# An MoE layer's 64 experts written out instead of looped, eleven weight buffers instead of eight, and row gathers signalled by pairs

## The reference

```python
logits = x @ gate_weight.T;  scores = softmax(logits)          # 64 experts in 8 groups of 8
# 3 groups with the highest maxima, then the 6 best experts inside them
slot = flat * C + jnp.minimum(pos, C - 1)                       # C = 96 rows per expert
buf = jnp.zeros((E * C, H)).at[slot].set(x[tok]).reshape(E, C, H)
g = einsum('ech,emh->ecm', buf, Wg);  u = einsum('ech,emh->ecm', buf, Wu)   # M = 176
out = einsum('ecm,ehm->ech', silu(g) * u, Wd)
y = sum(out[slot] * topk_w) + silu(x @ Sg.T) * (x @ Su.T) @ Sd.T
```

## Time and profile before

| what | before |
|---|---|
| three runs | 1605.34, 1607.7, 1599.73 us; median 1605.34 |
| the profiled execution's own time | 1592.39 us |
| its span, first to last instruction | 1590.4 us |
| mean granted TensorE clock | 0.932 |

### The profile page before, as it was taken

How to read it: one execution, slowest core, us unless ns; L and a number is a source line. 1 busy time by engine, 2 the same in 40 slices (tenths; PEclk the granted TensorE clock), 3 DMA queues, 4 the chain that set the end, 5 groups by cost and what they waited for, 6 DMA issues and landing times. The chain is left out here.

```text
span 1590.4 us, 35813 instructions
## 1 busy us (share of the span) xinstructions
PE 1382.2 (87%) x13732; PEld 971.8 (61%) x13733; DVE 1121.4 (71%) x2131; ACT 676.9 (43%) x1430; POOL 737.9 (46%) x811
## 2 busy tenths in 40 slices
PE   3849999997679999999999999999986976999832
PEld 2424545445546777777777777777765545888731
DVE  4867888876767898788878887887764687222229
ACT  1226777772144555555555555555541110222200
POOL 0341111100338697667666766676650027677610
PEclk9968999999779999999999999999997888999965
DMA  3052000000116988788788887887783300799838
GB/s 107 1 233 86 2 2 2 2 2 1 54 51 126 160 154 142 142 152 152 140 137 155 146 145 135 157 142 145 136 151 109 92 1 15 232 281 281 256 121 266
DMA packets 423530, 191.39 MB, mean 120 GB/s; under 512 B 377507, under 2 KB 397697, under 8 KB 423249
## 3 DMA queue, kind: packets, MB, share of 16 engines
q1 hardware_dynamic: 404576, 164.08, 49.1%
q0 software_dynamic: 6144, 12.52, 2.7%
q10 hardware_dynamic: 12656, 12.72, 2.5%
HBM read 73.91 MB, written 23.13 MB: 61 GB/s over the span
## 5 line engine op out<-in xcount | busy, mean ns | idle before, releaser
L941 POOL CAST a_ph<-a_p 128x1024 f16<-128x1024 f32 (+7 forms) x256 | 248.8, 972 | 232.4 <-ACT a_p L1087 232.3
L1137 DVE TENSOR_TENSOR a_ph<-a_p,a_ph 128x1024 f16<-128x1024 f32 (+7 forms) x256 | 259.6, 1014 | 14.5 <-POOL a_ph L941 14.4
L1087 ACT ACTIVATE a_p<-bank,a_negm 128x1024 f32<-128x1024 f32 (+7 forms) x256 | 188.9, 738 | 125.3 <-DVE a_negm L1154 124.9
L1047 PE MATMUL bank<-a_v,a_pt 128*128 128x128 f16 x3456 | 234.8, 219 | 4.6 <-DMA a_pt<-a_ph 4.4
L1029 PE MATMUL bank<-a_k,a_q 128*128 128x512 f16 (+3 forms) x1152 | 229.1, 326 | 7.8 <-ACT a_p L1087 7.1
L1047 PEld LDWEIGHTS bank<-a_v,a_pt 128*128 128x128 f16 x3456 | 211.0, 98 | 36.1 <-issue 3.5
L1154 DVE TENSOR_REDUCE a_negm<-bank 128x1 f32<-128x1024 f32 (+7 forms) x256 | 189.9, 742 | 25.7 <-PE bank L1034 24.1
L972 PE MATMUL bank<-x_part,wsplit 128*128 128x512 f16 x768 | 189.1, 384 | 1.8 <-PEq L182 1.8
L686 ACT ACTIVATE a_p<-bank 128x1024 f32<-128x1024 f32 x192 | 152.9, 809 | 68.0 <-PE bank L571 57.1
L1029 PEld LDWEIGHTS bank<-a_k,a_q 128*128 128x128 f16 x1152 | 98.8, 98 | 69.0 <-ACT a_p L1087 8.9
L706 DVE TENSOR_REDUCE a_max<-bank 128x2 f32<-128x1024 f32 (+3 forms) x128 | 128.8, 1022 | 17.0 <-PE bank L571 14.5
(11 more groups left out here) (206 smaller groups left out, 2441.5 us busy)
## 6 DMA issues: line engine op xcount, KB each, us to landing
wgu<-in_wgu SPq DMA_DIRECT2D x64, 352.0 KB
choice_rows<-zero SPq DMA_DIRECT2D x24, 512.0 KB, 5.8
wh<-in_wqkv SPq DMA_DIRECT2D x32, 384.0 KB, 3.9
c_rows<-choice_rows ACTq DMA_DIRECT2D x16, 768.0 KB
wd<-in_wd SPq DMA_DIRECT2D x64, 176.0 KB
a_pt<-a_ph SPq DMA_TRANSPOSE x256, 3.8
x<-in_x SPq DMA_DIRECT2D x1, 2048.0 KB, 9.3
wo<-in_wo SPq DMA_DIRECT2D x1, 2048.0 KB, 10.1
```

What stands on the lines that cost most here:

```text
L941: pool.tensor_copy(halves[j][:, :, 0, :], probs[j % 2][:, 0:blocks[j] * P].rearrange("p (n q) -> p n q", q=P)).then_inc(h_ready, 1)
L1047: ins = pe.matmul(V_ps[j % 2][:, 0:DH1], turned[j][:, 2 * q + a, :], vs[n % 2][v_][:, q, :], start=(q == 0 and (a, v_) == PARTS[0]), stop= ...
L1087: act.activation(probs[j % 2][:, 0:w_], S_ps[j % 2].rearrange("p a n -> p (a n)")[:, 0:w_], ACT.Exp, bias=negm[:, n % 2, j:j + 1], accum_o ...
L1137: dve.tensor_tensor(halves[j][:, :, 1, :], probs[j % 2][:, 0:blocks[j] * P].rearrange("p (n q) -> p n q", q=P), halves[j][:, :, 0, :], ALU ...
```

## The change

It has seven parts.

1. `experts` has no `Fori`: all 64 experts are written out on PE, ACT, DVE and SP, with waits on constants. The conditions that were met in advance by `nop` instructions are left out.
2. `XB` is 11: eleven buffers for weights, filled in the router block; SP's fetch for expert e waits for `down(e - 11)`. Buffers for rows keep their number, eight (`XR`).
3. The first eight gathers stand at the end of POOL's list in `router`, behind a wait for the instruction that writes `src` (`s_src`).
4. Rows are signalled by pairs: four semaphores of two experts each, and `turn_pair(j)` waits for its own pair.
5. POOL's wait for the zeros moves to the block `l0_ffn`, and the buffer `zero` is freed before the second attention layer, which makes room for the weights.
6. The shared expert's buffer `shared_g` shares memory with `slot`.
7. The four LayerNorm blocks share eight semaphores instead of having eight each; the values waited for are offset by constants.

```diff
@@ router @@
-    sg = [g.sb(f"shared_g{i}", [P, 512], F32, c) for i in range(2)]
+    sg = [slot.rearrange("p t e -> p (t e)")[:, i * 512:(i + 1) * 512] for i in range(2)]
...
-            dve.tensor_copy(g.src[:, :], picked[:, 0, :])
+            dve.tensor_copy(g.src[:, :], picked[:, 0, :]).then_inc(s_src, 1)
...
-            pool.wait_ge(g.s_zero, 16 * ZD)
+            pool.wait_ge(s_src, 1)
+            for e in range(XR):
+                gather_rows(g, pool, e)
...
+def gather_rows(g, pool, e):
+    pool.indirect_dma_start(out=g.rows[:, e % XR, :], out_offset=None, in_=g.xrows,
+                            in_offset=bass.IndirectOffsetOnAxis(ap=g.src[:, e:e + 1], axis=0),
+                            bounds_check=T - 1, oob_is_err=False).then_inc(g.s_row[e // 2 % (XR // 2)], 16)
@@ experts @@
         def _(sp):
-            with sp.Fori(1, E // XB) as i:
-                for s in range(XB):
-                    sp.wait_ge(s_dn, i * XB + (s - XB + 3))
...
+            for e in range(XB, E):
+                sp.wait_ge(s_dn, e - XB + 1)
+                sp.dma_start(g.wgu[e % XB][:, :, :], g.t["wgu"][e]).then_inc(g.s_wgu[e % XB], 16)
+                sp.dma_start(g.wd[e % XB][:, :, :], g.t["wd"][e]).then_inc(g.s_wgu[e % XB], 16)
...
         def _(pool):
-            for e in range(XB):
-                gather(e)
             for e in range(E):
-                if e + XB < E:
+                if e + XR < E:
                     pool.wait_ge(s_t, e // 2 + 1)
-                    gather(e + XB)
-                pool.wait_ge(s_o, e + 3)
+                    gather_rows(g, pool, e + XR)
+                pool.wait_ge(s_o, e + 1)
...
-            def turn_pair(p_num, s):
-                if s % XG == 0:
-                    pe.wait_ge(s_row[s // XG], p_num * (2 * ROWS_IN // XB) + (ROWS_IN - ROWS_IN * s // XB))
-                pe.wait_ge(s_tc, p_num + 1)
+            def turn_pair(j):
+                pe.wait_ge(g.s_row[j % (XR // 2)], 32 * (j // (XR // 2) + 1))
+                if j >= 2:
+                    pe.wait_ge(s_tc, j - 1)
...
-            with pe.Fori(0, E // XB - 1) as i:
-                one_pass(i, True)
-            one_pass(E // XB - 1, False)
+            turn_pair(0)
+            gu(0)
+            for e in range(E):
+                if e % 2 == 0 and e + 2 < E:
+                    turn_pair(e // 2 + 1)
+                if e + 1 < E:
+                    gu(e + 1)
+                down(e)
```

More of the change, by code:

```diff
@@ L160, in norm @@
 def norm(nc, g, tag, kind, loads=None, pool_work=None):
-    s_st, s_ag, s_sq, s_ch = [g.sem(f"{tag}_{n}") for n in ("stats", "aggr", "sqrt", "chain")]
-    s_xn, s_tr = g.sem(f"{tag}_xn"), g.sem(f"{tag}_tr")
-    s_ev = [g.sem(f"{tag}_evac{i}") for i in range(2)]
+    s_st, s_ag, s_sq, s_ch, s_xn, s_tr = [g.sem(f"norm_{n}") for n in ("stats", "aggr", "sqrt", "chain", "xn", "tr")]
+    s_ev = [g.sem(f"norm_evac{i}") for i in range(2)]
+    turn = int(tag[1])
+    ag0, sq0, ch0, xn0, tr0, ev0 = NT * turn, g.norm_sqrt, g.norm_chain, NT * turn, NT // 2 * turn, NT // 4 * turn
     s_hi = g.sem(f"{tag}_hi") if kind == "split" else None
@@ L1719, in down @@
                                     start=(m == 0), stop=(m == 1))
                 ins.then_inc(s_dn, 1)
-            pe.nop().then_inc(s_gu, 4)
-            pe.nop().then_inc(s_dn, 2)
-            turn_pair(0, 0)
-            gu(0, 0, 0)
-            def one_pass(i, more):
-                for s in range(XB):
-                    if s % 2 == 0 and (more or s + 2 < XB):
-                        turn_pair(i * (XB // 2) + (s // 2 + 1), (s + 2) % XB)
-                    if more or s + 1 < XB:
-                        gu(i * XB + (s + 1), (s + 1) % XB, i * (XB // 2) + (s + 1) // 2)
-                    down(i * XB + s, s)
@@ L1788, in _ @@
+            silu(0)
+            for e in range(E):
+                if e + 1 < E:
+                    silu(e + 1)
+                out_rows(e)
+            for i in range(NR):
+                act.wait_ge(s_out[i], 16 * (E // XG // NR))
         @block.vector
         def _(dve):
-            dve.nop().then_inc(s_tc, 2)
-            dve.nop().then_inc(s_h, 2)
-            def turned(p_num, s):
-                dve.wait_ge(s_t, p_num + 1)
-                dve.wait_ge(s_gu, p_num * 2 + 2)
-                dve.tensor_copy(xeT[(s // 2) % 2].rearrange("p a c n -> p (a c n)"),
-                                g.bank[0][:, (s // 2) % 2, 0:2 * DC * C]).then_inc(s_tc, 1)
@@ new lines, in product @@
+            def product(e):
+                dve.wait_ge(s_sil, e + 1)
+                if e >= 2:
+                    dve.wait_ge(s_dn, e - 1)
+                dve.tensor_tensor(h[e % 2][:, :, :], g.bank[1][0:MH, e % 2, 2 * C:4 * C].rearrange(
+                    "p (m c) -> p m c", c=C), sg[e % 2][:, :, :], ALU.mult).then_inc(s_h, 1)
+            turned(0)
+            product(0)
+            for e in range(E):
+                if e % 2 == 0 and e + 2 < E:
+                    turned(e // 2 + 1)
+                if e + 1 < E:
+                    product(e + 1)
@@ L1816, in combine @@
     s_g = g.s_wgu
-    EXPERTS = 32 * (E // XB)
+    EXPERTS = [32 * len(range(i, E, XB)) for i in range(NB)]
     s_acc, s_st, s_l, s_mm = g.sem("c_acc"), g.sem("c_store"), g.sem("c_last"), g.sem("c_mm")
```

172 lines of the change are left out of this document (79 added, 93 removed).

## The result

| what | before | after |
|---|---|---|
| median of seven runs, us | 1605.34 (1596.64 to 1613.25) | 1588.19 (1583.19 to 1592.02) |
| ratio, with its 95% interval | | 0.9898 [0.9871, 0.9924] |
| the profiled execution's own time, us | 1592.39 | 1592.02 |
| its span, us | 1590.4 | 1590.2 |

The kernel is 1.0% faster: 17.15 us by the medians, 16.4 by the ratio. I had forecast 8. The two profiled executions say 0.4 us.

The account below looks back on a forecast made before the run. The prediction took POOL's list of gathers and scatters as the bound, with PE having to keep up. Its terms, -11.0 + 3.6 - 0.6 = -8.0 us, took the median 1605.34 to about 1597 us, range 1589 to 1608.

Parts of the forecast that it names:

- P0 to the last scatter: Experts' block, from PE's first transpose (P0): with waits by pairs the last scatter starts at P0 + 162.3, before 173.3: -11.0 us.
- `src` to P0: Router's end, from the table of rows written to PE's first transpose: eight gathers and a drain before the barrier, +3.6 us.
- exit behind the last scatter: End of the experts' block, last scatter to ACT's next instruction: the drain stands behind 120 transfers, not 128, -0.6 us.
- rival E: Experts' block: it gives more, by landing in 1.64 us and a free drain, or a stall going with the loop; 1590 to 1594; 0.06.
- The chain of three pairs: Experts' block, gather through PE's output to scatter: 12.4 us against POOL's 15.2, so POOL isn't held up, 2.8 us to spare.
- The end of the block: Last experts: `turn_pair(31)` waits for expert 63's rows, at P0 + 152.8; then 9.49 us of PE's work to the last scatter.
- Rival C: Experts' block: the DMA engines become the bound, gathers land at 7.5 us or later, sum about -2, 1603 us; chance 0.10.
- Early gathers and the drain: Router's end: gathers start earlier but POOL then sets the barrier; drain 0.075 us per transfer, P0 at 1353.5, +3.6 us.
- rival B: POOL's drain has a fixed price of 9.63 us, so early gathers cost 12.7: +1.7 in all, 1607 us; chance 0.17.
- Eleven buffers: Weights in router and experts' blocks: PE showed no wait for weights, so three more buffers change nothing, 0 us.
- written out: Experts' block without the loop: register instructions go, but POOL, the bound, had none; more instruction fetches; 0 us.
- Rival D: Experts' block: slower, since instruction fetches for the written-out code stop PE; over 1613 us; chance 0.05.

Follow-up runs that it names:

- second profile of before: The kernel before, unchanged, run and profiled again: ratio 0.999 to before, median 1601.47 us; the profiled execution took 1607.78 us.
- by fours: The kernel after, but PE waits for both pairs of a group of four before transposing the first: ratio 1.0023 to before, median 1606.48 us.

## Why the prediction was off

The forecast was 1597 us, the result 1588.19, below the range's 1589. The sum fits the profile that it was made from. Carrying it over to the median was wrong.

| term | said | profile after against profile before | against the second profile of before |
|---|---|---|---|
| P0 to the last scatter | -11.0 | 173.26 to 162.80: -10.5 | 182.15 to 162.80: -19.4 |
| `src` to P0 | +3.6 | 10.76 to 13.41: +2.65 | 10.84 to 13.41: +2.6 |
| exit behind the last scatter | -0.6 | 12.41 to 11.76: -0.65 | 12.42 to 11.76: -0.65 |
| sum | -8.0 | -8.5 | -17.4 |

**The step that failed** is the first one under "The change part by part": "The sum is made against the profiled execution (span 1590.4 us, own time 1592.39 us), which is 12.95 us below the median of the three runs", and "I carry the difference over to that median". That holds only if the difference sits in work that both kernels share. A large part of it did not: the unchanged kernel's second profile has 10.0 us more between the scatters, and by pairs this stage took 153.0 to 154.0 us in all seven profiles with weights fetched. The right reckoning was from a stage that varies to POOL's own pace. With the two profiles of before as ends, the change is worth 8.5 to 17.4 us, and the measured 16.4 lies near the upper end. The median run was not profiled. An estimate of its stage comes from the ratios: each changed kernel's four lengths, plus its gain, less the other three lengths of before, leave 168 to 172 us, and not 163.3.

The term behind it that the prediction put at nothing is the clock. It priced POOL's standing from a profile with a granted clock of 1.00 from 1359.5 to 1504. The second profile has four falls to 0.50 in this stage, 1.7 us of PE's work each. They go with waits of 1.8 to 2.5 us for rows, and by pairs, where no wait behind the first turn is above 1.3 us, there are none. How often they come in the executions that were not profiled stays open.

I had the number in hand. A profile 12.95 us under the median, with 14.3 us of POOL's standing in the changed stage, should have made rival E a wide case, up to -11.0 - 12.95 + 3.0 = -21, and not 6 in 100 down to 1590.

Point by point:

- *Rows by pairs* is the whole gain, shown from both sides: by fours the changed kernel loses it (1.0023), by pairs alone the kernel before has it (0.9892).
- *The chain of three pairs* did not close. The last waited turn shows the landing time: the gather of expert 57 was issued by 1492.89 + 0.98 = 1493.87, and PE turned at 1499.73, 5.86 us later. Over the nine waited turns it is 5.7 to 6.3, more than the 4.75 I allowed, but with the 2.8 us to spare it closes only at 7.5.
- *The end of the block* came out right in part by luck. The prediction has PE's last turn wait for expert 63, at P0 + 152.8; it came at P0 + 153.32. But the last wait for rows was that of turn 28, at 1499.73, and PE came to the last turn at its own pace, 14.43 us for three pairs. The rows of expert 63 had 5.08 us to land and PE didn't wait for them. Two paths of nearly the same length gave the same sum.
- *Rival C* was right about the load, 0.98, and wrong about its effect: PE's waits are 3.3 us and cost POOL nothing. Its sum was loose as well: with half of the 14.3 us left, the scatters would take 156.2 us and the sum be about -4, not -2. The price of the load is the last 3.3 us (153.73 against 150.39), at the end of the block.
- *Early gathers and the drain.* 13.41 us, where I had 1353.5 - 1339.10 = 14.4. The eight issues took what I said; from the last one to P0 it was 2.28 us, where I had laid landing, drain and barrier end to end at 3.4. The small price per transfer held (0.05 to 0.08 us, where I had 0.075), and rival B (one fixed price) is refuted. But I costed this edit against a kernel that waits for four gathers. Beside rows by pairs it waits only for two, and the early gathers are then a loss of 5.2 us, not 3.6: the two edits take from each other.
- *The trap in the Trainium skill* ("SBUF — State Buffer", section on the two sides of SBUF), by which GpSimd could not write its DMAs' descriptors beside VectorE's 2-port copies. In the first fence of the result DVE works from 1348.65 to 1350.29 beside gathers of 1.31 and 0.97 us, as long as those with DVE idle. No delay shows, and so far the sum was right to go by the rows. But this instruction reads PSUM (`bank`), and no run shows whether it is a copy of the kind that the page means. So the trap is not refuted here.
- *Eleven buffers* at 0 and *written out* at 0 held: 0.9904 with eight, 154.00 us of scatters with the loop left. Rival D is refuted too. Nine instruction fetches came in 130 us (below), and PE's waits in the middle are those for rows.

The DMA queues of the kernel after, 1370 to 1500 (packets, MB, share of 16 engines):

```profile
q1 hardware_dynamic: 12218, 27.25, 70.1%
q0 software_dynamic: 4763, 9.73, 27.0%
q8 instruction: 9, 0.15, 0.5%
```

## What to carry to other kernels

Before a difference is carried from one profiled execution to a median, ask in which stage the two differ. Where the change takes away waits that depend on how fast loaded DMAs land, the median may hold many more of them than a quick profile shows, and the range has to reach that far. Read the granted clock behind each wait too: a wait can cost a second time when the clock falls behind it. Signal buffers in the units in which they are consumed, and move ahead of a barrier only what the first consumer needs: two gathers there brought PE's start 2.7 us nearer (too little for the measured times to tell), eight put it off by 5.2 us.

## What the runs showed of the hardware

A gather of 96 rows that PE waited for landed 1.62 to 1.76 us after its issue with the DMA share at 0.28 or less, and 3.4 to 6.5 us after it in stretches with a mean share of 0.86 to 0.98. The Trainium skill ("DMA: Bandwidth & Descriptors", section on latency and other measured facts) says that access to HBM goes from 0.2 us on average to 2 us at high load and that lighter load makes a transfer's fixed cost smaller. The direction agrees. The growth measured here, up to 4.9 us, is more than that alone; what else is in it no run here shows.

POOL's drain at the end of the experts' block costs 0.082 us for each DMA that POOL issued in it: 10.4 us behind 126, though without the drain the next block started 1.89 us after the last issue, with every scatter landed. Behind eight gathers it costs 0.3 us more than behind two. No engine works meanwhile, so no row names it; only the gap between two blocks shows it.

TensorE's granted clock fell from 1.00 to 0.50 (from its 2.4 to its 1.2 GHz level) for 3.4 us at a time, four times in the second profile of before and twice in that by fours. Each time PE had just stood idle 1.8 to 2.5 us for rows. Sixteen matmuls of one expert took 2.72 us at 0.50 and 1.49 us at 1.00. Idle times of 2.00 and 2.27 us without a fall stand beside them, so the length of the wait alone does not decide it here.
